# Macaron block: flag 2 summed in a gate bank, tile 2's norm moved to GpSimd with its own loads, the first norm in halves, and new orders on every engine

## The chip, the cores and the metric

One core of a Trainium2 chip. The metric is the device time of the kernel in microseconds (us); lower is better. The kernel before was run three times: 368.39, 368.41 and 369.13 us, median 368.41 us.

## What is computed

The input is 4096 tokens of 128 features (16 sequences of 256). Two feed-forward halves stand around an attention-like pooling, each with a residual and each behind a norm over the features:

```python
def ffn(x):                       # weights are -1, 0 or 1, with a scale per output
    h = silu(tlin(x, w1)) * tlin(x, w2)        # 128 -> 512, twice
    h = gelu(tlin(h, h1))                      # 512 -> 512
    h = gelu(tlin(h, h2))                      # 512 -> 512
    return tlin(h, w3)                         # 512 -> 128
x = x + 0.5 * ffn(layernorm(x))
h = layer_norm(layernorm(x), gamma, beta)      # keys, values, logits: 128 x 128
w = exp(key_att / sqrt(128)); w = w / cumsum(w, axis=1)
x = x + cumsum(w * keys, axis=1) * values
x = x + 0.5 * ffn(layernorm(x))
```

## The kernel before, in words

Tokens are cut into 8 tiles of 512. The feed-forward network runs 16 times: T = 0 to 7 is the first half, T = 8 to 15 the second, and `a0` to `a7` are the attention of the tiles between them. Activations stand with features on the partitions and tokens along the row, so one matmul has 128 x 512 moving elements. Each activation is split into a rounded part and its rest (`hi` and `lo`), and every product is two matmuls, one with each part, on a rounded copy of the weights.

The layers are called by the names that stand in the orders: `p1.m` is block m of the first layer (four matmuls: gate with hi and lo, up with hi and lo), `p2.m` and `p3.m` a block of the two 512-wide layers (8 matmuls), `p4` the last layer (8). ScalarE (ACT) computes `tanh`, `gelu2`, `gelu3` and the hi parts `high1` to `high3`; VectorE (DVE) computes `gate` and `up` (the silu product) and the lo parts `low1` to `low3`; GpSimd (POOL) takes the two lo parts `low1.1` and `low1.2` of the first tile and rounds the weights of h1, h2 and w3 (`hi`).

**Orders.** No scheduler runs. Each engine follows a list written out by hand: `START` has the stages before and during the first layer of tile 0, `SECOND_LAYER` has the matmuls of tile 0's second layer one by one (`p2ahi.0` is input block a, hi part, output block 0), and `STEPS` has 16 further steps. A prefix such as `0:` or `a1:` names another tile than the step's own. Every engine runs its list in order, so an instruction that waits holds all behind it.

**Norms.** Tiles 0, 1 and 2 (`BY_PE`) are normalised in the layout with tokens on partitions: DVE takes statistics (`stats`, `aggr`, `veps`), POOL the roots (`norm`, a power), ACT (for tile 0 mostly DVE) forms `z`, and four transposes on TensorE (PE) turn it (`t`). All other tiles go another way: POOL aggregates the statistics (`aggregate`), SP sends means and roots to DRAM (`park`) and back, spread over all partitions (`wide`), and POOL adds and multiplies (`xn.0`, `xn.1`) on the transposed input `xt_sb`, which arrives by one 2 MB load.

**Flags.** The kernel has two versions of each matmul, on rounded and on raw weights, and decides at run time: the low bits of the weights are looked at (`bits`), their maxima are summed over partitions by a 1-wide matmul (`flag:sum`), DVE copies the sum (`flag:copy`), and PE's sequencer loads it and branches. There are three such branches: before the first layer of tile 0, before its second layer, and before the rest. In this data the flags are 0. The sum of flag 2 is written in `y_ps`, which `p1.3` of tile 0 needs afterwards, so it stands between `p1.1` and `p1.2`, and `p1.3` waits for its copy:

```python
def flag_home(part):
    return (hid_ps[0], y_ps, xt_ps)[part - 1][0:1, 0:1]
...
if (T, m) in ((0, 3), (1, 1)):
    eng.wait_ge(s_flag, T + 2)
```

**Ahead of the first layer** PE runs seven `warm_up` matmuls on ones (two passes each): four at once, two after the variances (`s_ve`), one after the roots (`s_pow`); then the sum of flag 1 and the transposes of tile 0.

Of the kernel before, what the change touches and what calls it, by code (L numbers as in the profile page):

```python
# [36 lines left out]
    "DVE": (  # L37
        "stats aggr veps bits:w1 bits:w2 norm",
        "flag:copy1 bits:h1.0 t vec:scales bits:h1.2 stats flag:raise2 aggr gate.0 veps flag:copy2 up.0 gate.1 "
        "up.1 low1.0 gate.2 up.2 gate.3 up.3 bits:h2.1 low1.3 1:t",  # L40
# [32 lines left out]
        "a1:norm norm a1:xn.0 a0:weight a1:xn.1 xn.0 xn.1",
        "norm a0:dt xn.0 xn.1",
        "a2:norm a1:weight norm a2:xn.0 a2:xn.1 a1:dt xn.0 xn.1",
        "a3:norm norm a3:xn.0 a3:xn.1 a2:weight xn.0 xn.1",
        "a2:dt norm a4:norm xn.0 xn.1",
        "a3:weight norm a4:xn.0 a4:xn.1 xn.0 xn.1",
        "a5:norm a3:dt a4:weight a5:xn.0 a5:xn.1 norm a4:dt xn.0 xn.1",
# [1138 lines left out]
```

## Time and profile before

| | |
|---|---|
| median of three runs | 368.41 us |
| the profiled execution | 368.15 us |
| its span | 366.4 us |
| mean granted TensorE clock | 0.998 of full |
| PE busy | 359.3 us, 98% |
| DVE, ACT, POOL busy | 316.2, 283.1, 163.3 us |

A busy PE is not PE at its peak, since matmuls overlap and their ends are modelled; what shows a loss is the distance from one start to the next. The span lies 1.75 us below the execution's own time, and that rest lies outside of the profiled instructions.

### The profile page before, as it was taken

To read this page: it belongs to the slowest core of one execution; us is meant where nothing else is said; L and a number is where in the kernel's file an instruction comes from. 1 tells how busy PE (TensorE), PEld (TensorE's weight loads), DVE (VectorE), ACT (ScalarE), POOL (GpSimd) and SP (SyncE) were. 2 spreads that over 40 slices of the span, in tenths; PEclk is the share of its full clock that TensorE was granted. 3 is DMA by queue.
4 is the path that set the end of the run, shared out by engine and by line. 5 is a ranking of instruction groups with operands and counts; after the bars stand their busy time and mean duration, and the time that the engine had idled before them with its cause. 6 is when DMAs were issued, how large, how long until landed. Compare 5 with 4: busy or idle time off the path is not lost.

```text
span 366.4 us, 5194 instructions
## 1 busy us (share of the span) xinstructions
PE 359.3 (98%) x1578; PEld 285.1 (78%) x1578; DVE 316.2 (86%) x550; ACT 283.1 (77%) x465; POOL 163.3 (45%) x251
## 2 busy tenths in 40 slices
PE   7999999999999999999999999999999999999996
PEld 2678888787877777788778787787778777888885
DVE  5999688999989998889899989998899799857642
ACT  4998777987777879776887968877897697686763
POOL 3553344649045565812685545652573740530000
PEclk9999999999999999999999999999999999999999
DMA  7770103030100301300222012012022020040001
GB/s 245 270 294 4 54 3 107 8 110 9 58 2 0 86 29 36 83 0 2 59 59 59 1 59 59 0 59 86 0 59 88 2 86 2 4 111 2 1 30 63
DMA packets 16256, 20.94 MB, mean 57 GB/s; under 512 B 7008, under 2 KB 8288, under 8 KB 15968
## 3 DMA queue, kind: packets, MB, share of 16 engines
q1 hardware_dynamic: 15504, 19.75, 18.2%
q10 hardware_dynamic: 720, 0.80, 0.7%
q8 instruction: 16, 0.26, 0.3%
q14 instruction: 16, 0.13, 0.1%
HBM read 18.36 MB, written 2.18 MB: 56 GB/s over the span
## 4 chain that ended last, share of the span: by engine, by line
PE 96%; DVE 2%; issue 1%; ACT 1%; POOL 0%; POOLq 0%; ACTq 0%
PE hid_ps L643 62%; PE gate_ps L643 8%; PE y_ps L643 8%; PE up_ps L643 7%; PE y_ps L662 2%; PE xt_ps L829 2%; PE xt_ps L833 2%; PE xt_ps L836 2%; PE y_ps L843 1%; PE gate_ps L707 1%; PE up_ps L707 1%; DVE gate L1070 0%; PE xt_ps L643 0%; DVE xt_sb L1142 0%; PE xt_ps L656 0%
## 5 line engine op out<-in xcount | busy, mean ns | idle before, releaser
L643 PE MATMUL hid_ps<-act_hi,hi_h 128*128 128x512 f32 x480 | 193.3, 403 | 0.0
L643 PE MATMUL hid_ps<-act_lo,hi_h 128*128 128x512 f32 x480 | 186.7, 389 | 0.0
L1092 DVE TENSOR_TENSOR act_lo<-full,act_hi 128x512 fp32r<-128x512 f32 x185 | 132.8, 742 | 23.6 <-ACT act_hi L909 20.6
L902 ACT ACTIVATE full<-hid_ps,vec 128x512 f32<-128x512 f32 x123 | 84.1, 687 | 57.2 <-PE hid_ps L643 51.7
L643 PEld LDWEIGHTS hid_ps<-act_hi,hi_h 128*128 128x128 f32 x480 | 90.3, 188 | 22.8 <-issue 2.6
L643 PEld LDWEIGHTS hid_ps<-act_lo,hi_h 128*128 128x128 f32 x480 | 90.2, 188 | 21.3 <-issue 2.6
L909 ACT ACTIVATE act_hi<-full 128x512 fp32r<-128x512 f32 x127 | 78.6, 628 | 1.6
L567 POOL TENSOR_TENSOR xnt<-xt_sb,wide 128x512 f32<-128x512 f32 x21 | 29.4, 1400 | 45.8 <-DMA wide<-rows 45.8
L885 ACT ACTIVATE tanh<-gate_ps,s_half 128x512 f32<-128x512 f32 x60 | 40.4, 680 | 7.4 <-PE gate_ps L643 7.3
L1070 DVE SCALAR_TENSOR_TENSOR gate<-tanh,gate_ps 128x512 f32<-128x512 f32 x60 | 40.3, 674 | 6.5 <-ACT tanh L885 6.4
L1082 DVE SCALAR_TENSOR_TENSOR full<-up_ps,s_half,gate 128x512 f32<-128x512 f32 x60 | 44.1, 741 | 1.1
L890 ACT ACTIVATE act_hi<-full 128x512 fp32r<-128x512 f32 x60 | 36.9, 625 | 1.9 <-DVE full L1082 1.7
L573 POOL TENSOR_TENSOR xnt<-xnt,wide 128x512 f32<-128x512 f32 x21 | 30.0, 1428 | 3.2 <-POOL xnt L567 0.4
L622 POOL TENSOR_TENSOR xt_sb<-xt_sb,adelta 128x512 f32<-128x512 f32 x8 | 12.3, 1532 | 42.7 <-DVE adelta L1174 42.7
L540 POOL TENSOR_TENSOR pair_diff<-stats 128x4 f32<-128x4 f32 x21 | 8.2, 388 | 44.2 <-DVE stats L1040 44.2
L1158 DVE RECIPROCAL rcsum<-csum 128x256 f32<-128x256 f32 x16 | 27.8, 1740 | 0.0
L553 POOL TENSOR_TENSOR pair<-veps,half 128x4 f32<-128x4 f32 x21 | 26.1, 1244 | 3.3 <-POOL veps L550 0.4
L643 PE MATMUL gate_ps<-xn_hi,hi_w 128*128 128x512 f32 x59 | 25.1, 425 | 0.3 <-ACT full L902 0.3
L643 PE MATMUL y_ps<-act_hi,hi_w 128*128 128x512 f32 x60 | 23.8, 396 | 0.0
L643 PE MATMUL y_ps<-act_lo,hi_w 128*128 128x512 f32 x60 | 23.4, 390 | 0.0
L643 PE MATMUL gate_ps<-xn_lo,hi_w 128*128 128x512 f32 x59 | 23.0, 391 | 0.0
L643 PE MATMUL up_ps<-xn_hi,hi_w 128*128 128x512 f32 x59 | 23.0, 390 | 0.0
(170 smaller groups left out, 440.3 us busy)
## 6 DMA issues: line engine op xcount, KB each, us to landing
wide<-rows SPq DMA_DIRECT2D x42, 256.0 KB, 3.7
xt_sb<-xt SPq DMA_DIRECT2D x1, 2048.0 KB, 10.6
out<-xt_sb SPq DMA_DIRECT2D x7, 256.0 KB, 4.0
x_sb<-x SPq DMA_DIRECT2D x1, 1536.0 KB, 6.8
raw_h<-h2t SPq DMA_DIRECT2D x4, 256.0 KB, 7.1
raw_h<-h1t SPq DMA_DIRECT2D x2, 256.0 KB, 6.1
rows<-pair SPq DMA_DIRECT2D x21, 4.0 KB, 2.2
raw_w<-w2t ACTq DMA_DIRECT2D x1, 256.0 KB, 4.0
```

The costliest lines, as they stand in the source:

```text
L553: eng.tensor_tensor(pair_b[q][:, 1, :], veps[:, :], half[:, :], ALU.pow).then_inc(s_pow, 1)
L567: eng.tensor_tensor(xnt_b[i][:, :], xt_tile(t), wide_b[i][:, 0:TOK], ALU.add).then_inc(s_centred, 1)
L573: eng.tensor_tensor(xnt_b[i][:, :], xnt_b[i][:, :], wide_b[i][:, TOK:2 * TOK], ALU.mult).then_inc(s_xn, 1)
L643: mm = eng.matmul(ps, w, a, start=(first and n == 0), stop=(last and n == len(seq_) - 1))
L885: eng.activation(tanh_b[m % 2][:, :], gate_home(T, m)[:, :], ACT.Tanh, scale=s1_half[:, m:m + 1]).then_inc(s_tanh, 1)
L890: eng.activation(act_hi[first_act(T)][:, m, :], full1[m % 2][:, :], ACT.Copy).then_inc(s_hi[1], 1)
L902: eng.activation(full23[m % 2][:, :], home23(n, T, m)[:, :], ACT.Gelu, scale=col("sh1" if n == 2 else "sh2", m)).then_inc(s_gelu[n], 1)
L909: eng.activation(act_hi[n][:, m, :], full23[m % 2][:, :], ACT.Copy).then_inc(s_hi[n], 1)
L1070: eng.scalar_tensor_tensor(gate_b[m % 2][:, :], tanh_b[m % 2][:, :], 1.0, gate_home(T, m)[:, :], ALU.add, ALU.mult).then_inc(s_gate, 1)
L1082: eng.scalar_tensor_tensor(full1[m % 2][:, :], up_home(T, m)[:, :], s12_half[:, m:m + 1], gate_b[m % 2][:, :], ALU.mult, ALU.mult).then_in ...
L1092: eng.tensor_tensor(act_lo[a][:, m, :], full[m % 2][:, :], act_hi[a][:, m, :].bitcast(F32), ALU.subtract).then_inc(s_lo[n], 1)
L1158: eng.reciprocal(rcsum[:, b], csum[:, b]).then_inc(s_rc, 1)
```

## The change

- **Flag 2.** Its sum goes to `gate_ps[0]`, behind all of `p1.0` to `p1.3`, and waits for the first `gate` instead of `xn_lo`. `p1.3` of tile 0 no longer waits for a flag.
- **Tile 2.** `BY_PE` is now (0, 1): tile 2 goes by POOL, park and wide. Its `x` and its part of `xt` have loads and semaphores of their own, ahead of the rest; the other parts of `xt` follow in two loads.
- **First norm.** Aggregation, variances and roots of tile 0 are made in two halves, and DVE's `z` blocks wait for their half alone.
- **Weights.** The rounding of h2 and w3 on POOL is now part of the orders.
- **Orders.** All lists are written anew.

```diff
-        "p1.0 p1.1 flag:sum2 p1.2 p1.3",
+        "p1.0 p1.1 p1.2 p1.3 flag:sum2",
...
-        "hi:w1 hi:w2 z",
-        "t vec:s1 bits:h1.1 bits:h1.3 tanh.0 tanh.1 tanh.2 high1.0 tanh.3 high1.1 z.0 z.1 high1.2 bits:h2.0 "
-        "high1.3 1:t",
+        "hi:w1 hi:w2 z 0:t vec:s1",
+        "tanh.0 tanh.1 bits:h1.1 tanh.2 bits:h1.3 bits:h2.0 high1.0 tanh.3 high1.1 z.0 high1.2 z.1",
...
     "POOL": (
-        "norm",
-        "norm xn.0 xn.1",
+        "hi:h2.0 hi:h2.1 hi:h2.2 norm hi:h2.3 xn.0 xn.1",
+        "hi:w3 norm xn.0 xn.1",
...
-BY_PE = (0, 1, 2)
-AGGREGATE = 3
+BY_PE = (0, 1)
+AGGREGATE = 2
...
-            return (hid_ps[0], y_ps, xt_ps)[part - 1][0:1, 0:1]
+            return (hid_ps[0], gate_ps[0], xt_ps)[part - 1][0:1, 0:1]
...
-            xload(2, NT, s_xr)
+            xload(2, 3, s_x2t)
+            eng.dma_start(xt_tile(2), xt[:, 2 * TOK:3 * TOK]).then_inc(s_xt2, 16)
+            xload(3, NT, s_xr)
...
-            eng.dma_start(xt_sb[:, :], xt).then_inc(s_xt, 16)
+            eng.dma_start(xt_sb[:, 0:2 * TOK], xt[:, 0:2 * TOK]).then_inc(s_xt, 16)
+            eng.dma_start(xt_sb[:, 3 * TOK:], xt[:, 3 * TOK:]).then_inc(s_xt, 16)
...
+            def first_norm():
+                for h, ready, done in ((0, s_ve_first, s_pow_first), (1, s_ve, s_pow)):
+                    cut = slice(h * SUB // 2, (h + 1) * SUB // 2)
+                    eng.wait_ge(ready, 1)
+                    eng.tensor_tensor(rstd[:, cut], veps[:, cut], half[:, cut], ALU.pow).then_inc(done, 1)
+                eng.wait_ge(s_pow_first, 1)
+                eng.wait_ge(s_pow, 1)
+                eng.tensor_tensor(nmr[:, :], neg_mean[:, :], rstd[:, :], ALU.mult).then_inc(s_nmr, 1)
...
-                if (T, m) in ((0, 3), (1, 1)):
-
-                    eng.wait_ge(s_flag, T + 2)
+                if (T, m) == (1, 1):
+
+                    eng.wait_ge(s_flag, 3)
...
                 if part == 2:
-                    eng.wait_ge(s_xlo_half, 2)
+                    eng.wait_ge(s_gate, 1)
...
-                eng.wait_ge(s_pow, 1)
                 for j in range(SUB - act_z(0)):
+                    eng.wait_ge(*((s_pow_first, 1) if j < SUB // 2 else (s_pow, 1)))
```

What stands on PE in the first layer of tile 0. Before, from its second block to its end (the 1-wide matmul is the sum of flag 2):

```order
L643 MATMUL up_ps<-xn_hi,hi_w 128x512
L643 MATMUL up_ps<-xn_lo,hi_w 128x512
L764 MATMUL y_ps<-ones,inexact 1x1
L643 MATMUL hid_ps<-xn_hi,hi_w 128x512
L643 MATMUL hid_ps<-xn_lo,hi_w 128x512
```

Now, at the section's end (the branch to the flag's load follows at once):

```order
L659 MATMUL xt_ps<-xn_hi,hi_w 128x512
L659 MATMUL xt_ps<-xn_lo,hi_w 128x512
L780 MATMUL gate_ps<-ones,inexact 1x1
L871 UNCONDITIONAL_BRANCH
```

The sum moved from the middle of the section to behind its last product. On DVE, from the copy of flag 1 (`flag_i<-hid_ps`) to the copy of flag 2 (`flag_i<-y_ps`), before:

```order
L1027 CAST flag_i<-hid_ps 1x1
L1012 TENSOR_REDUCE bits<-raw_h 128x1
L1122 TENSOR_TENSOR xn_lo<-xt_ps,xn_hi 128x256
L1122 TENSOR_TENSOR xn_lo<-y_ps,xn_hi 128x256
...
L1012 TENSOR_REDUCE bits<-raw_h 128x1
L1040 BN_STATS stats<-x_sb 128x6 x4
L1022 TENSOR_REDUCE inexact<-bits 128x1
L1045 MEMSET fence 128x1
L1047 BN_AGGR mv<-stats 128x2 x4
L1070 SCALAR_TENSOR_TENSOR gate<-tanh,gate_ps 128x512
L1054 TENSOR_SCALAR neg_mean<-mv 128x4
L1055 TENSOR_SCALAR veps<-mv 128x4
L1027 CAST flag_i<-y_ps 1x1
```

Now, behind both `xn_lo`, up to the copy of flag 2 (`flag_i<-gate_ps`):

```order
L1026 TENSOR_REDUCE bits<-raw_h 128x1
L1013 TENSOR_SCALAR s_half<-vec 128x1
L1015 TENSOR_TENSOR s_half<-s_half,vec 128x4
L1026 TENSOR_REDUCE bits<-raw_h 128x1
L1090 SCALAR_TENSOR_TENSOR gate<-tanh,gate_ps 128x512
L1057 BN_STATS stats<-x_sb 128x6 x4
L1102 SCALAR_TENSOR_TENSOR full_0<-up_ps,s_half,gate 128x512
L1062 MEMSET fence 128x1
L1064 BN_AGGR mv<-stats 128x2 x4
L1036 TENSOR_REDUCE inexact<-bits 128x1
L1090 SCALAR_TENSOR_TENSOR gate<-tanh,gate_ps 128x512
L1041 CAST flag_i<-gate_ps 1x1
```

The first look at h1's bits moved behind `xn_lo`, and `up.0` and a second `gate` came in ahead of the copy. On ACT, behind tile 0's `xn_hi`, up to the first hi part of the activations. Before:

```order
L914 ACTIVATE keys,bits<-raw_h 128x512
L914 ACTIVATE csum,bits<-raw_h 128x512
L885 ACTIVATE tanh<-gate_ps,s_half 128x512 x2
L885 ACTIVATE tanh<-hid_ps,s_half 128x512
L890 ACTIVATE act_hi<-full_0 128x512
```

Now:

```order
L899 ACTIVATE tanh<-gate_ps,s_half 128x512 x2
L928 ACTIVATE keys,bits<-raw_h 128x512
L899 ACTIVATE tanh<-hid_ps,s_half 128x512
L928 ACTIVATE csum,bits<-raw_h 128x512
L928 ACTIVATE rcsum,bits<-raw_h 128x512
L904 ACTIVATE act_hi<-full_0 128x512
```

The two looks at h1's bits moved behind the first `tanh`, and a look at h2's bits came in ahead of `act_hi`.

## Rows read from the trace of the kernel before

**Rows 1.** Busy time of each engine in three stretches, with granted clock.

```profile
8.60:13.60 5.00, 4.45 (x22) 3.06 (x22) 4.96 (x22) 4.10 (x11) 2.96 (x5) 1.00 0.75 280
13.60:25.40 11.80, 11.49 (x50) 8.41 (x50) 11.24 (x29) 11.36 (x24) 7.44 (x9) 1.00 0.89 335
50.00:150.00 100.00, 100.00 (x434) 80.11 (x433) 93.61 (x154) 81.84 (x131) 55.64 (x91) 1.00 0.15 43
```

**Rows 2.** Timeline of PE, first layer: start us, duration, instruction, idle before.

```profile
6.65 0.81 PE L843 MATMUL y_ps<-ones 128*1 128x256 f32 x3
...
8.69 0.36 PE L678 MATMUL gate_ps<-xn_hi,hi_w 128*128 128x256 f32 x1 [0.56 <-ACT xn_hi L968]
...
10.42 0.40 PE L643 MATMUL up_ps<-xn_lo,hi_w 128*128 128x512 f32 x1
...
11.22 0.50 PE L643 MATMUL hid_ps<-xn_hi,hi_w 128*128 128x512 f32 x1
...
13.04 0.39 PE L643 MATMUL xt_ps<-xn_lo,hi_w 128*128 128x512 f32 x1
13.64 0.47 PE L707 MATMUL gate_ps<-act_hi,hi_h 128*128 128x512 f32 x1 [0.22 <-ACT act_hi L890]
```

**Rows 3.** Load of flag 1 by PE's sequencer: durations in ns, start.

```profile
L856 PEldq TENSOR_LOAD <-flag_i x1: 492/492/492, 7.8 to 7.8; - x1
```

**Rows 4.** Timeline of DVE, from the first variances to the second gate.

```profile
5.18 1.27 DVE L1012 TENSOR_REDUCE bits<-raw_w 128x1 f32<-128x512 uint16 x2
...
7.58 0.15 DVE L1027 CAST flag_i<-hid_ps 1x1 int32<-1x1 f32 x1 [0.30 <-PE hid_ps L756]
...
8.70 0.41 DVE L1122 TENSOR_TENSOR xn_lo<-y_ps,xn_hi 128x256 fp32r<-128x256 f32 x1
...
9.46 0.68 DVE L1012 TENSOR_REDUCE bits<-raw_h 128x1 f32<-128x512 uint16 x1
10.12 0.87 DVE L1040 BATCH_NORM_STATS2 stats<-x_sb 128x6 f32<-128x128 f32 x4
...
12.76 0.66 DVE L1070 SCALAR_TENSOR_TENSOR gate<-tanh,gate_ps 128x512 f32<-128x512 f32 x1
```

**Rows 5.** Timeline of ACT: a look at bits of h1.

```profile
8.88 0.63 ACT L914 ACTIVATE keys<-raw_h 128x512 f32<-128x512 uint16 x1 [0.18 <-DMA raw_h<-h1t]
```

**Rows 6.** Timeline of POOL: a power, and the rounding of h2.

```profile
5.36 1.02 POOL L578 TENSOR_TENSOR rstd<-veps,half 128x4 f32<-128x4 f32 x1 [3.30 <-DVE veps L1055]
...
18.27 2.76 POOL L584 CAST hi_h<-raw_h 128x512 fp32r<-128x512 f32 x4
```

**Rows 7.** Timeline of PE: first layer of tile 1, tile 2's transposes.

```profile
25.50 0.47 PE L643 MATMUL gate_ps<-xn_hi,hi_w 128*128 128x512 f32 x1 [0.32 <-ACT full L902]
...
26.86 0.49 PE L643 MATMUL hid_ps<-act_hi,hi_h 128*128 128x512 f32 x1
...
30.63 0.60 PE L656 MATMUL xt_ps<-ident,z 128*128 128x128 f32 x4
30.98 0.48 PE L643 MATMUL hid_ps<-act_hi,hi_h 128*128 128x512 f32 x1
```

**Rows 8.** Tile 3's norm: first and last of the aggregation, `xn.0`, `xn.1`.

```profile
30.02 0.21 POOL L540 TENSOR_TENSOR pair_diff<-stats 128x4 f32<-128x4 f32 x1 [4.71 <-DVE stats L1040]
...
32.07 1.04 POOL L553 TENSOR_TENSOR pair<-veps,half 128x4 f32<-128x4 f32 x1
...
38.73 1.29 POOL L567 TENSOR_TENSOR xnt<-xt_sb,wide 128x512 f32<-128x512 f32 x1 [5.62 <-DMA wide<-rows]
40.17 1.56 POOL L573 TENSOR_TENSOR xnt<-xnt,wide 128x512 f32<-128x512 f32 x1
```

**Rows 9.** SP's issues of the load of `xt` and of tile 3's first `wide`.

```profile
16.05 0.45 SPq L486 DMA_DIRECT2D xt_sb<-xt  x1
...
34.73 0.34 SPq L503 DMA_DIRECT2D wide<-rows  x1
```

**Rows 10.** Issues of DMA by line: KB each, us from issue to landing.

```profile
xt_sb<-xt SPq DMA_DIRECT2D x1, 2048.0 KB, 10.6
```

More of the change, by code:

```diff
@@ L29 @@
         "flag:sum1 t",
-        "p1.0 p1.1 flag:sum2 p1.2 p1.3",
+        "p1.0 p1.1 p1.2 p1.3 flag:sum2",
     ),
     "ACT": (
-        "hi:w1 hi:w2 z",
-        "t vec:s1 bits:h1.1 bits:h1.3 tanh.0 tanh.1 tanh.2 high1.0 tanh.3 high1.1 z.0 z.1 high1.2 bits:h2.0 "
-        "high1.3 1:t",
+        "hi:w1 hi:w2 z 0:t vec:s1",
+        "tanh.0 tanh.1 bits:h1.1 tanh.2 bits:h1.3 bits:h2.0 high1.0 tanh.3 high1.1 z.0 high1.2 z.1",
     ),
     "DVE": (
-        "stats aggr veps bits:w1 bits:w2 norm",
-        "flag:copy1 bits:h1.0 t vec:scales bits:h1.2 stats flag:raise2 aggr gate.0 veps flag:copy2 up.0 gate.1 "
-        "up.1 low1.0 gate.2 up.2 gate.3 up.3 bits:h2.1 low1.3 1:t",
[4 rows of a table added]
     ),
@@ L51 @@
     "SP": (
-        "",
+        "park wide",
         "park wide",
         "a0:park a0:wide park wide",
-        "a1:park park a1:wide wide",
-        "park wide",
-        "a2:park park a2:wide wide",
+        "a1:park a1:wide park",
+        "park 5:wide wide",
+        "a2:park a2:wide park wide",
         "a3:park a3:wide park wide",
@@ L62 @@
         "park wide",
-        "a6:park 8:store a6:wide park wide",
-        "a7:park a7:wide 9:store park wide",
-        "10:store park 11:store wide store",
+        "a6:park a6:wide park wide",
+        "a7:park a7:wide park 8:store wide",
+        "park 9:store 10:store 11:store wide store",
         "store",
@@ L69 @@
     "POOL": (
-        "norm",
-        "norm xn.0 xn.1",
+        "hi:h2.0 hi:h2.1 hi:h2.2 norm hi:h2.3 xn.0 xn.1",
+        "hi:w3 norm xn.0 xn.1",
         "a0:norm norm a0:xn.0 a0:xn.1 xn.0 xn.1",
[L73 to L79, printed above, removed]
+        "a1:norm norm 6:norm a1:xn.0 a0:weight a1:xn.1 xn.0 xn.1",
+        "a0:dt a1:weight xn.0 xn.1",
+        "a2:norm norm a2:xn.0 a2:xn.1 xn.0 a1:dt xn.1",
+        "a3:norm norm a3:xn.0 a2:weight a3:xn.1 xn.0 xn.1",
+        "a2:dt norm a4:norm a3:weight xn.0 xn.1",
+        "norm a4:xn.0 a4:xn.1 a3:dt xn.0 xn.1",
+        "a5:norm a4:weight a5:xn.0 a5:xn.1 norm a4:dt xn.0 xn.1",
         "norm a5:weight xn.0 xn.1",
@@ L304, in macaron_block @@
         s_x0_half, s_xt = sem("s_x0_half"), sem("s_xt")
+        s_x2t, s_xt2 = sem("s_x2t"), sem("s_xt2")
         s_h1 = [sem(f"s_h1_{k}") for k in range(MC)]
@@ L387, in items @@
                     yield stage, chunk, int(which) if which else i + AHEAD.get(stage, 0)
-        norm_of = {("ffn", t): t for t in range(2)}
-        for i, order in enumerate(STEPS["DVE"]):
+        norm_of = {}
+        for i, order in enumerate(START["DVE"] + STEPS["DVE"], -2):
             for stage, _, t in items(order, i):
                 if stage in ("stats", "att_stats"):
-                    norm_of["ffn" if stage == "stats" else "att", t] = len(norm_of)
+                    norm_of.setdefault(("ffn" if stage == "stats" else "att", t), len(norm_of))
         assert len(norm_of) == 3 * NT
@@ L562, in xn_add @@
                     eng.wait_ge(s_x1, t + 1)
+                elif t == 2:
+                    eng.wait_ge(s_xt2, 16)
                 elif t < NT:
-                    eng.wait_ge(s_xt, 16)
+                    eng.wait_ge(s_xt, 32)
                 else:
@@ L592, in low1 @@
                                   ALU.subtract).then_inc(s_lo[1], 1)
-            norm(0)
+            first_norm()
             eng.wait_ge(s_z, SUB - 1)
@@ L602, in _ @@
                     low1(stage)
-            for k in range(MC):
-                hi("h2", k)
-            hi("w3", 0)
             def emit(stage, chunk, t):
-                if stage in ("norm", "att_norm"):
+                if stage == "hi":
+                    hi(t, chunk or 0)
+                elif stage in ("norm", "att_norm"):
                     kind = "ffn" if stage == "norm" else "att"
@@ L796, in emit @@
                             return
-                        free("xt", (s_xlo, t))
-                        transpose4(xt_ps, z, s_t)
                     elif stage == "p4":
@@ L1027, in copy_flag, with blocks_of, norm_stats @@
                 eng.tensor_copy(flag_i[0:1, part - 1:part], home).then_inc(s_flag, 1)
-            def norm_stats(kind, t):
+            def blocks_of(half):
+                return range(SUB) if half is None else range(half * SUB // 2, (half + 1) * SUB // 2)
+            def norm_stats(kind, t, half):
                 n = norm_of[kind, t]
@@ L1036, in norm_stats @@
                     eng.wait_ge(s_nmr, n - LINES + 1)
-                for j in range(SUB):
+                for j in blocks_of(half):
                     if (n, j) == (0, SUB // 2):
@@ L1040, in norm_stats, with norm_aggr, norm_veps @@
                     eng.bn_stats(stats_b[n % LINES][:, j, :], norm_blk(kind, t, j)).then_inc(s_bn, 1)
-            def norm_aggr(n):
-                eng.wait_ge(s_bn, SUB * n + SUB)
+            def norm_aggr(n, half):
+                eng.wait_ge(s_bn, SUB * n + blocks_of(half)[-1] + 1)
                 eng.memset(fence[:, :], 0.0)
-                for j in range(SUB):
+                for j in blocks_of(half):
                     eng.bn_aggr(mv[:, j, :], stats_b[n % LINES][:, j, :]).then_inc(s_mv, 1)
-            def norm_veps(n):
-                eng.wait_ge(s_mv, SUB * n + SUB)
+            def norm_veps(n, half):
+                js = blocks_of(half)
+                cut = slice(js[0], js[-1] + 1)
+                eng.wait_ge(s_mv, SUB * n + js[-1] + 1)
                 if n > 0:
                     eng.wait_ge(s_nmr, n)
-                eng.tensor_scalar(neg_mean[:, :], mv[:, :, 0], -1.0, None, ALU.mult)
-                eng.tensor_scalar(veps[:, :], mv[:, :, 1], 1.0, EPS, ALU.mult, ALU.add).then_inc(s_ve, 1)
+                eng.tensor_scalar(neg_mean[:, cut], mv[:, cut, 0], -1.0, None, ALU.mult)
+                eng.tensor_scalar(veps[:, cut], mv[:, cut, 1], 1.0, EPS, ALU.mult,
+                                  ALU.add).then_inc(s_ve_first if half == 0 else s_ve, 1)
             def first_norm():
-                eng.wait_ge(s_pow, 1)
                 for j in range(SUB - act_z(0)):
+                    eng.wait_ge(*((s_pow_first, 1) if j < SUB // 2 else (s_pow, 1)))
                     eng.tensor_scalar(z[:, j * P:(j + 1) * P], norm_blk("ffn", 0, j), mv[:, j, 0:1], rstd[:, j:j + 1],
@@ L1145, in emit @@
                     if t == 0:
-                        eng.wait_ge(s_xt, 16)
+                        eng.wait_ge(s_xt, 32)
                     eng.wait_ge(s_p4, t + 1)
```

13 lines of the change are left out of this document (7 added, 6 removed), and 184 rows, old and new, of tables (SECOND_LAYER, START, STEPS).

## The prediction

> **What bounds the kernel now.** I read the page first, then the busy time by stretches. From 50 to 150 us PE is busy for 100.00 of 100.00 us at the full clock [rows 1], and the two stretches of 100 us behind it read the same. So no engine but PE can give time there, and no order can: what is left to gain is in the start. In the first 5 us of the first layer PE is busy for 4.45, while DVE is for 4.96; from 13.60 to 25.40 PE lacks 0.31 of 11.80 [rows 1]. The end time is therefore PE's fixed work plus PE's pauses, nearly all of them ahead of 26 us, and I sum pauses.
>
> The reader is to see these in PE's timeline [rows 2]. A 512-wide matmul starts 0.23 behind the one before it. From 10.42 to 11.22 there are 0.80, so 0.57 are lost at the sum of flag 2. From 13.04 to 13.64 there are 0.60, so 0.37 are lost at the first `act_hi`. Ahead of 8.69 the warm-up matmuls run without a gap up to about 7.46 (0.81 from 6.65), and the flag's sum and the transposes follow. The copy of flag 1 ends at 7.58 + 0.15 = 7.73 [rows 4], the load of it begins at 7.8 and takes 0.49 [rows 3], and the first matmul comes at 8.69: 0.96 from copy to matmul, although `xn_hi` was there earlier. A flag read with nothing queued on PE behind it costs this 0.9 to 1.0. The Trainium skill (DMA: Bandwidth & Descriptors, Latency and other measured facts) gives such a load a floor of about 600 ns; this trace's 0.49 is below it, so the row stands, and by the page the sum at the end would be 0.1 more. Later, at 25.50, PE waits once more, for ACT [rows 7].
>
> **The first norm in halves: +0.1.** The start of `z` is not bound by the roots alone: DVE looks at w1 and w2 until 5.18 + 1.27 = 6.45, and the power ends at 5.36 + 1.02 = 6.38 [rows 4, 6]. The change puts a memset and two short instructions more ahead of these looks, with a wait between them. I take 0.3 to 0.4 for it, from the distance of such instructions (the aggregation to the looks at 5.18), so `z` comes at 6.8 instead of 6.4. PE doesn't care: its warm-ups hold it until 7.46. But the second part of the warm-ups waits for the variances, whose semaphore now comes 0.3 later; it had some 0.1 of slack. What I add is 0.1. The cost of a power on half the columns isn't in the trace: between nearly nothing and the whole 1.02 [rows 6]. I take about 0.6, since four columns took 1.02 and POOL's other instructions on as few columns take 0.2, so most of it goes with the columns. At the whole price, twice, the last warm-up waits until 7.4 and the start comes 0.4 later; below zero there is nothing, since the warm-ups stand.
>
> **Flag 2: the pause moves and grows, +1.5 at the start of the second layer.** The 0.57 at 10.42 go. `p1.3` then ends its issue at 12.5 instead of 13.3. But the read of flag 2 was hidden before: its copy stood ahead of `up.0` and so ahead of the second gate at 12.76 [rows 4], while PE had matmuls until 13.04 [rows 2]. Now nothing is queued on PE behind the sum. So I follow DVE, which copies it, in its new order. Both `xn_lo` end at 8.70 + 0.41 + 0.1 = 9.2. Then: look at h1 0.67, scales 0.4, look 0.67 (the distance from 9.46 to 10.12), which gives 10.95; gate 0.66; statistics 0.8 (the row's 0.87 ends 0.1 into the next instruction), `up` 0.7, aggregation 0.35, raise 0.1: 13.5; the second gate 0.66 and the copy: 14.25 [rows 4]. The first `tanh` is no bound (done at 10.6, as its bank is done at 9.9). On ACT the looks at h1 come behind the `tanh`s (0.63 each, with 0.78 to the next start [rows 5]); the last ends at 13.3, just ahead of the raise. From the copy 0.85 to 0.95 to PE's first matmul (the 0.96 above; two waits follow the branch): 15.1. `act_hi` isn't later: a look at h2 from 13.3, then `act_hi` until 14.7. So the second layer starts at 15.1 against 13.64, and behind the DVE's queue are `veps`, `up.1` and `low1.0`, which come 1 us later too.
>
> **From there to the second layer's end: +1.0 left.** Fewer pauses are left, because PE comes later than its inputs. I went through the new list with steps of 0.23: `low1.0` is done at 15.8 for its place at 15.9, POOL's `low1.1` at 17.3 for 17.8, `z` at 18.6 for 18.9, `low1.2` at 19.2 for 19.4. All are in time by 0.1 to 0.5. PE reaches tile 1's `p1.3` at 26.7; its banks are free when two `gelu2` are done, which stand on ACT behind the `tanh` of `p1.1`'s bank (24.8, three times 0.68): 26.9. Before it was 25.50 [rows 7], so +1.4. The fold's matmuls, which stood between 26.4 and 26.86, now lie ahead of `p1.3` and no longer behind it. So the first `p3` comes at 27.85 against 26.86 [rows 7]: +1.0.
>
> **Tile 2's transposes: -0.4.** Four starts from 30.63 to 30.98 go, 0.35 [rows 7], and the matmul behind transposes is a little slow. ACT is rid of four `z` (1.6 us), DVE of `aggr` and `veps`; both are off PE's path there, which is worth nothing with PE at 100%.
>
> **Tile 2 by POOL: 0.** Its chain is: `low1.2` until 19.2, three roundings of 0.69 (2.76 for four [rows 6]) until 21.3, aggregation 3.1 (30.02 to 33.11 [rows 8]) until 24.4. Then park. Tile 3 took 1.6 from the end of its power to the first `wide` (34.73 [rows 9]) and 4.0 more to `xn.0` at 38.73 [rows 8]. But the load of `xt` runs from 16.05 to 26.65 (10.6 [rows 9, 10]), and park is issued in the midst of it. I take it to land as that load ends: `wide` at 27.0, `xn.0` 31.0, `xn.1` done 34.0 (3.0 for both [rows 8]), ACT's `xn_hi` 34.6, `xn_lo` 35.3. PE wants the one at 27.85 + 4 x 1.81 = 35.1 and the other at 35.3. So it just fits; the bounds are 0 and 1.2. The roundings of h2 that wait behind the aggregation end at 25.1, ahead of the first `p3`.
>
> **All other orders: 0**, with bounds 0 and +0.8: PE is full there, so a new order can only bring a wait in.
>
> **The sum.** +1.0 - 0.4 + 0 = +0.6, of which +0.1 is the norm's. Against the profiled execution, 368.15 (span 366.4 and 1.75 around it), that is 368.7. The median of the runs is 0.26 above that execution, so 368.9 to 369.0; I take 368.9. A measurement of this kernel can tell about 0.2% (0.7 us) from no change.
>
> **A: as summed, 45%.** Own range 368.3 to 369.7, since the start at 15.1 is known to about 0.3 and the stretch behind it to 0.4. The bound of 0.2% at 369.15 cuts it: same 27, slower 18.
>
> **B: a new wait at tile 2 or in the orders, 20%.** Place: `p1.0` of tile 2, at 35 us. It decides if park's 4 KB wait longer than until 26.65 or if `wide` needs more than 4.0. Each us of lateness is one of PE's: 0.7 to 1.5 more, so 369.6 to 370.4. For it: 0.0 to 0.1 of slack in my sum. Against it: landing without the load's queue would be a us sooner. The Trainium skill (DMA: Bandwidth & Descriptors, section Two DMAs through the same engine are not ordered) says that descriptors of one queue start in order, which speaks for this rival, since park would start behind the whole load.
>
> **C: faster, 20%.** The second layer starts at 13.7 or sooner. Place: the copy of flag 2 on DVE. It decides if that copy ends by 12.9 instead of 14.25. Then the pauses of 0.57 and 0.37 are gone for good, the transposes' 0.4 and part of the wait at 25.50 too: 1.0 to 1.4 less, 367.0 to 367.4. For it: all the gaps that it closes are there [rows 2]. Against it: DVE was busy for 4.96 of 5.00 us [rows 1], and `up` and a second gate were put ahead of the copy. Faster 18, same 2.
>
> **D: PE's clock falls in the pause, 5%.** PE stands still from 12.9 to 15.1, 2.2 us, where it never stood longer than 0.6 behind the warm-ups [rows 2]; the granted clock was full all along [rows 1]. At the lower of its two levels, 1.2 instead of 2.4 GHz, each us of the time costs half a us. I take 4 us for it, a guess below the 6.65 by which the warm-ups had brought it up [rows 2], so 2 us: 370.9. The Trainium skill (TensorE: Matmul & The Clock Gate, What's actually happening) has the clock follow PE's recent activity, which is this rival's ground.
>
> **E: half a power costs a whole one, 5%.** 0.4 more: 369.3, slower 4, same 1. **F: no effect, 5%.** The flag's gain and its price cancel, 367.6 to 368.4: same 4, faster 1. Of B, 18 are slower and 2 the same.
>
> Together, rounded: faster (18 + 1) 0.20, same (27 + 2 + 2 + 1 + 4) 0.35, slower (18 + 18 + 5 + 4) 0.45. The range: 367.4 to 370.6; it leaves out the better half of C and D, and the end of B.
>
> **What would show it.** Right: no gap at 10.4; the second layer's first matmul at 15.1; `p1.3` of tile 1 at 26.9; the first `p3` at 27.9; no transposes at 31; PE full from 28 us on. Wrong: a copy of flag 2 ahead of 13.5; a flag read under 0.7; a wait of PE at 35 us on `xn_hi` or `xn_lo`; a granted clock under 1 at 15 us; waits of PE behind 50 us.

## The result: 369.84 us against 368.40, and the profile after

Over 12 runs each the changed kernel takes 369.84 us in the median (368.62 to 370.80), the kernel before 368.40 (367.54 to 369.58): a ratio of 1.0038, interval 1.0029 to 1.0047, so 1.4 us slower. The profiled execution took 369.77 us with a span of 368.0, 1.6 more than before's.

The first view is PE's timeline, cut to the places that matter: start, duration, instruction, idle time ahead.

```profile
9.15 0.35 PE L694 MATMUL gate_ps<-xn_hi,hi_w 128*128 128x256 f32 x1 [0.60 <-ACT xn_hi L982]
...
12.69 0.39 PE L659 MATMUL xt_ps<-xn_lo,hi_w 128*128 128x512 f32 x1
13.63 0.19 PE L780 MATMUL gate_ps<-ones,inexact 128*1 128x1 f32 x2 [0.55 <-DVE inexact L1036]
14.87 0.47 PE L723 MATMUL gate_ps<-act_hi,hi_h 128*128 128x512 f32 x1 [1.05 <-ACT act_hi L904]
...
26.75 0.47 PE L659 MATMUL gate_ps<-xn_hi,hi_w 128*128 128x512 f32 x1
...
27.75 0.39 PE L659 MATMUL hid_ps<-act_hi,hi_h 128*128 128x512 f32 x1
...
35.02 0.39 PE L659 MATMUL gate_ps<-xn_hi,hi_w 128*128 128x512 f32 x1
35.52 0.50 PE L659 MATMUL gate_ps<-xn_lo,hi_w 128*128 128x512 f32 x1
...
332.28 0.41 PE L659 MATMUL gate_ps<-xn_hi,hi_w 128*128 128x512 f32 x1
332.86 0.50 PE L659 MATMUL gate_ps<-xn_lo,hi_w 128*128 128x512 f32 x1 [0.17 <-DVE xn_lo L1147]
```

Against [rows 2]: the first layer is dense now and ends at 12.69 instead of 13.04 although it begins 0.46 later, but the second begins 1.23 later, at 14.87. Against [rows 7]: the two places come 1.25 and 0.89 later. The transposes of tile 2 are gone, which gives back 0.44. Then come two waits that before doesn't have. At 35.02 and at 332.28 a matmul is followed by the next after 0.50 and 0.58 instead of 0.23. Both times it waits for `xn_lo`, of tile 2 and of the last tile.

To follow the loss further, count PE's matmuls back from the end in both traces and compare the starts of those with as much work behind them. The changed kernel is 0.30 later behind tile 2's place (0.89 at the first `p3`, less 0.44 for the transposes, less 0.15 since its matmuls lie a little closer there), 0.73 behind 35, 0.80 at 100, 1.20 behind a wait at 136.41 (DVE's `act_lo`), 1.33 from 225 on and 1.79 behind 332. That is the loss, by place: 0.3 in the start, 0.4 at tile 2, 1.1 in the other orders. Towards the end 0.17 comes back, which leaves the span's 1.6.

Next DVE's timeline of the changed kernel ahead of the second layer:

```profile
11.04 0.69 DVE L1090 SCALAR_TENSOR_TENSOR gate<-tanh,gate_ps 128x512 f32<-128x512 f32 x1 [0.16 <-ACT tanh L899]
11.65 0.86 DVE L1057 BATCH_NORM_STATS2 stats<-x_sb 128x6 f32<-128x128 f32 x4
12.43 0.73 DVE L1102 SCALAR_TENSOR_TENSOR full<-up_ps,s_half,gate 128x512 f32<-128x512 f32 x1
...
13.49 0.68 DVE L1090 SCALAR_TENSOR_TENSOR gate<-tanh,gate_ps 128x512 f32<-128x512 f32 x1
14.08 0.14 DVE L1041 CAST flag_i<-gate_ps 1x1 int32<-1x1 f32 x1
```

POOL's timeline of it for tile 2, from the casts of h2 to the first addition, and the same addition of the last tile:

```profile
18.98 2.19 POOL L602 CAST hi_h<-raw_h 128x512 fp32r<-128x512 f32 x3
21.14 0.20 POOL L547 TENSOR_TENSOR pair_diff<-stats 128x4 f32<-128x4 f32 x1
...
30.90 1.29 POOL L576 TENSOR_TENSOR xnt<-xt_sb,wide 128x512 f32<-128x512 f32 x1 [6.54 <-DMA wide<-rows]
...
328.63 1.29 POOL L576 TENSOR_TENSOR xnt<-xt_sb,wide 128x512 f32<-128x512 f32 x1 [7.17 <-DMA wide<-rows]
```

And SP's (the DMA queue's own; the second number is the time to issue), at tile 2 and at the last tile:

```profile
23.81 0.39 SPq L502 DMA_DIRECT2D rows<-pair  x1
27.43 0.34 SPq L510 DMA_DIRECT2D wide<-rows  x1
...
321.48 0.37 SPq L502 DMA_DIRECT2D rows<-pair  x1
321.90 1.44 SPq L520 DMA_DIRECT2D out<-xt_sb  x3
324.45 0.33 SPq L510 DMA_DIRECT2D wide<-rows  x1
```

The same places for the last tile in the kernel before, SP's issues and POOL's first addition:

```profile
319.10 0.37 SPq L495 DMA_DIRECT2D rows<-pair  x1
319.51 0.47 SPq L513 DMA_DIRECT2D out<-xt_sb  x1
320.70 0.32 SPq L503 DMA_DIRECT2D wide<-rows  x1
...
325.31 1.84 POOL L567 TENSOR_TENSOR xnt<-xt_sb,wide 128x512 f32<-128x512 f32 x1 [6.24 <-DMA wide<-rows]
```

The copy of flag 2 ends at 14.22 (14.25 in the prediction), and the matmul follows 0.65 behind it. From tile 2's park to its `wide` 3.62 us pass, from the last tile's 2.97, with three stores between the two. In the kernel before both took 1.6, tile 3's in [rows 9] and the last tile's here, with one store between.

### The profile page after: what moved, and what is told of

It reads as the page before. It is cut to its first block, busy times and chain, and to the rows that moved or that the text cites. A ratio compares the mean times of both kernels' runs of the same rounds, so it can differ in the third digit from the quotient of the medians.

```text
span 368.0 us, 5197 instructions
## 1 busy us (share of the span) xinstructions
PE 359.8 (98%) x1574; PEld 284.5 (77%) x1574; DVE 316.5 (86%) x546; ACT 281.6 (77%) x461; POOL 171.5 (47%) x260
## 4 chain that ended last, share of the span: by engine, by line
PE 84%; DMA 4%; POOL 4%; DVE 3%; issue 2%; ACT 2%; POOLq 0%; ACTq 0%; DVEq 0%; SPq 0%
PE hid_ps L659 54%; PE gate_ps L659 7%; PE y_ps L659 7%; PE up_ps L659 7%; PE y_ps L678 2%; DMA wide<-rows 2%; PE xt_ps L843 2%; PE xt_ps L847 2%; PE xt_ps L850 2%; DMA rows<-pair 2%; PE y_ps L857 2%; POOL xnt L576 1%; DVE act_lo L1112 1%; DVE gate L1090 1%; POOL hi_h L602 1%
## 5 line engine op out<-in xcount | busy, mean ns | idle before, releaser
L576 POOL TENSOR_TENSOR xnt<-xt_sb,wide 128x512 f32<-128x512 f32 x22 | 31.9, 1452 | 46.3 <-DMA wide<-rows 46.2
L582 POOL TENSOR_TENSOR xnt<-xnt,wide 128x512 f32<-128x512 f32 x22 | 30.9, 1406 | 2.7
L659 PE MATMUL gate_ps<-xn_hi,hi_w 128*128 128x512 f32 x59 | 25.9, 439 | 0.0
L659 PE MATMUL up_ps<-xn_lo,hi_w 128*128 128x512 f32 x59 | 23.0, 390 | 0.0
```

What stands on the lines that cost most here:

```text
L576: eng.tensor_tensor(xnt_b[i][:, :], xt_tile(t), wide_b[i][:, 0:TOK], ALU.add).then_inc(s_centred, 1)
L582: eng.tensor_tensor(xnt_b[i][:, :], xnt_b[i][:, :], wide_b[i][:, TOK:2 * TOK], ALU.mult).then_inc(s_xn, 1)
L659: mm = eng.matmul(ps, w, a, start=(first and n == 0), stop=(last and n == len(seq_) - 1))
```

## Experiments

Twelve kernels in four groups, each with the kernel before on the same chip (medians of before 368.50, 368.19, 368.48 and 368.17). Ratios are to before, with their 95% interval. Kernels that differ by one or two thousandths aren't told apart by their times; there the traces show which wait is there and which isn't.

### Parts of the change, one at a time

**Flag 2 alone.** Before, with only this, and the two waits that go with it (`p1.3` of tile 0 no longer waits for the flag, the sum waits for the first `gate`):

```diff
-        "p1.0 p1.1 flag:sum2 p1.2 p1.3",
+        "p1.0 p1.1 p1.2 p1.3 flag:sum2",
...
-            return (hid_ps[0], y_ps, xt_ps)[part - 1][0:1, 0:1]
+            return (hid_ps[0], gate_ps[0], xt_ps)[part - 1][0:1, 0:1]
...
-        "flag:copy1 bits:h1.0 t vec:scales bits:h1.2 stats flag:raise2 aggr gate.0 veps flag:copy2 up.0 gate.1 "
+        "flag:copy1 bits:h1.0 t vec:scales bits:h1.2 stats flag:raise2 aggr gate.0 veps up.0 gate.1 flag:copy2 "
```

> The kernel before with one thing moved: flag 2 is summed behind p1.3 in the first gate bank and copied behind gate.1; all orders else are before's. Theory (the flag's place costs little, what follows it costs): the 0.57 us gap at 10.42 goes, the copy lands near 13.3 and the second layer starts at 13.8 to 13.9 instead of 13.64, so the kernel is within 0.3 us of before (368.4 to 368.8). Rival (the late read itself is the loss of the changed kernel's start): the second layer starts at 14.7 or later and the kernel costs 0.9 us or more over before.

368.60 us, ratio 0.9995 (0.9983 to 1.0007). The second layer starts at 13.68, 5.06 behind the first matmul (4.95 before), and PE runs 0.39 ahead of before until 210; 0.33 of that is lost by 225. The theory holds, the late read is not the loss: with before's orders around it the copy is early enough, and the 0.57 at 10.42 and a wait of 0.22 for `act_lo` are gone.

**The first norm whole.** The changed kernel, one power on POOL again, for which all of DVE's `z` wait, and

```diff
-        "stats.0 stats.1 aggr.0 veps.0 aggr.1 veps.1 bits:w1 bits:w2 norm flag:copy1 0:t bits:h1.0 vec:scales",
+        "stats aggr veps bits:w1 bits:w2 norm flag:copy1 0:t bits:h1.0 vec:scales",
```

> The changed kernel with the first norm's aggregation, variances and roots whole again. Theory (the half norm makes the first matmul 0.46 us late, by a late variance semaphore and by powers of 0.69 us each): the first first-layer matmul starts near 8.7 instead of 9.15, and as the flag's copy and the act_hi behind it follow it, the kernel gets 0.3 to 0.45 us faster than the changed one (369.4 to 369.5). Rival (x landed 0.2 us later and the vector engine's order is what counts): the matmul stays at 8.95 or later, gain 0.2 us at most.

369.72 us, 1.0030 (1.0018 to 1.0042): no gain. The first matmul came at 8.41 and the second layer 0.74 sooner than in the changed kernel's trace, and then it was lost at once, as PE's timeline of this kernel shows:

```profile
12.89 0.19 PE L780 MATMUL gate_ps<-ones,inexact 128*1 128x1 f32 x2 [0.55 <-DVE inexact L1036]
14.13 0.47 PE L723 MATMUL gate_ps<-act_hi,hi_h 128*128 128x512 f32 x1 [1.04 <-ACT act_hi L904]
...
17.14 0.63 PE L723 MATMUL up_ps<-act_hi,hi_h 128*128 128x512 f32 x1
17.56 0.63 PE L723 MATMUL gate_ps<-act_hi,hi_h 128*128 128x512 f32 x1
17.99 0.63 PE L723 MATMUL gate_ps<-act_lo,hi_h 128*128 128x512 f32 x1
18.41 0.44 PE L723 MATMUL up_ps<-act_lo,hi_h 128*128 128x512 f32 x1
```

Matmuls start 0.43 apart instead of 0.23. The busy times by stretch of the same kernel say why (busy time and count of PE, PEld, DVE, ACT, POOL, then granted clock, DMA share, GB/s):

```profile
9.00:14.00 5.00, 3.53 (x19) 2.59 (x18) 4.87 (x21) 4.42 (x11) 1.40 (x4) 1.00 0.64 218
14.00:19.00 5.00, 4.87 (x14) 3.73 (x15) 4.93 (x11) 4.46 (x10) 4.20 (x6) 0.66 0.88 305
19.00:26.00 7.00, 7.00 (x35) 5.50 (x34) 4.85 (x10) 4.68 (x9) 4.30 (x11) 1.00 0.92 340
```

The granted clock is 0.66 over 14 to 19, so PE was at the lower of its two levels for more than half of that stretch, behind its pause from 12.35 to 14.13. PE went from 0.74 ahead of the changed kernel to 0.87 behind: 1.6 us. That is rival D, and it comes and goes between executions of one kernel (below). The first norm itself can't be priced from this time, so neither theory nor rival is decided.

**Flag 2 copied sooner**, by the orders:

```diff
-        "tanh.0 tanh.1 bits:h1.1 tanh.2 bits:h1.3 bits:h2.0 high1.0 tanh.3 high1.1 z.0 high1.2 z.1",
+        "bits:h1.1 tanh.0 tanh.1 bits:h1.3 tanh.2 high1.0 tanh.3 high1.1 z.0 high1.2 z.1 bits:h2.0",
-        "stats.0 stats.1 aggr.0 veps.0 aggr.1 veps.1 bits:w1 bits:w2 norm flag:copy1 0:t bits:h1.0 vec:scales",
-        "bits:h1.2 gate.0 stats up.0 aggr flag:raise2 gate.1 flag:copy2 veps up.1 low1.0 gate.2 up.2 gate.3 "
+        "stats.0 stats.1 aggr.0 veps.0 aggr.1 veps.1 bits:w1 bits:w2 norm flag:copy1 bits:h1.0 0:t vec:scales",
+        "bits:h1.2 stats gate.0 aggr up.0 flag:raise2 gate.1 flag:copy2 veps up.1 low1.0 gate.2 up.2 gate.3 "
```

> The changed kernel with flag 2 copied sooner: bits h1.1 go into ScalarE's 1.2 us of idle time ahead of the first tanh, bits h2.0 behind z, bits h1.0 into the vector engine's idle time ahead of xn_lo, up.0 and the flag ahead of the rest. Theory (the second layer waits for the copy and for an act_hi that stand behind checks which could lie elsewhere): the copy lands at 13.4 to 13.6 instead of 14.08, the second layer starts at 14.0 to 14.3 instead of 14.87, the kernel is 0.5 to 0.9 us faster than the changed one (368.9 to 369.3). Rival (what is won at the second layer's start is given back at its act_lo or its later flag): the start moves, p1.3 of tile 1 stays at 26.7, and the time stays at 369.8.

369.85 us, 1.0032 (1.0015 to 1.0050). The copy came at 13.07 and the second layer at 13.90, 4.93 behind the first matmul instead of 5.71, and `p3` at 27.08, not 27.75. But `xn_lo` of tile 2 was ready only at 35.1, so PE's matmul there came 0.52 late instead of 0.27, and about 0.6 were lost at 260 and 0.3 at 332. The theory was right on the start, which can be had from the orders. The rival was right on the time, since the gain was given back, but not on the place: `p1.3` of tile 1 did come sooner, and the loss is at tile 2, which doesn't follow, and behind.

**Part of `xt` later.** The 1280 KB transfer is issued behind tile 2's `wide`:

```diff
-            eng.dma_start(xt_sb[:, 3 * TOK:], xt[:, 3 * TOK:]).then_inc(s_xt, 16)
...
                     wide("ffn" if stage == "wide" else "att", t)
+                    if (stage, t) == ("wide", 2):
+                        eng.dma_start(xt_sb[:, 3 * TOK:], xt[:, 3 * TOK:]).then_inc(s_xt, 16)
```

> The changed kernel with the 1280 KB transfer of xt issued behind tile 2's wide rows instead of ahead of the steps. Theory (the park of tile 2 is slow since it shares the queues with that transfer): park to wide takes 1.6 to 2.5 us instead of 3.6, wide is issued 1 us or more sooner, PE's wait at 35 (0.38 us) goes, and the kernel is 0.3 to 0.4 us faster than the changed one (369.4 to 369.5). Rival (the park is slow whatever lies beside it, or the 3.6 us are the park's turn behind GpSimd): the wait at 35 stays within 0.1 us of what it is, and so does the time.

369.19 us, 1.0020 (1.0004 to 1.0036). Park to `wide` took 3.24 instead of 3.62, and the wait at 35 stayed (0.29). The theory was not confirmed. Only the 512 KB of `xt` were still under way when park was issued at 23.47, and they landed at 24.10, 2.6 before park did. So what held it is not seen here; the 1280 KB account for 0.4 at most.

### Tile 2 and the later orders

**The aggregation ahead of the casts**, in POOL's first step:

```diff
-        "hi:h2.0 hi:h2.1 hi:h2.2 norm hi:h2.3 xn.0 xn.1",
+        "norm hi:h2.0 hi:h2.1 hi:h2.2 hi:h2.3 xn.0 xn.1",
```

> The changed kernel with GpSimd's aggregation of tile 2 ahead of its three casts of h2 (2.2 us) instead of behind them. Theory (tile 2's xn is late since its aggregation stands behind casts that nothing waits for before 26.7): the park is issued near 21.7 instead of 23.8, tile 2's xn_lo is ready by 34, PE's wait at 35 (0.38 us) goes, the kernel is 0.3 to 0.4 us faster than the changed one. Rival (the path is bound by the DMA queues, which carry xt until 27.1): the park is issued earlier, the wide rows land at 30.5 to 30.9 all the same, and the wait at 35 stays.

369.59 us (7 runs), 1.0044 (1.0026 to 1.0062). Park was issued 2 us sooner, at 21.85, and `wide` at 26.56: 4.71 for 4 KB. PE's wait at 35 is gone in this trace, since `xn_lo` came 0.8 sooner, and the median didn't fall. In the kernels below with the same edit, both together and both with the earlier copy, the park took 5.51 and 6.83. However early it is issued, from 20.9 to 23.8, `wide` comes between 26.6 and 27.7. That is what the rival said of the queue, though the wait did not stay.

**Before's orders from step 4 on**: on all five engines the strings of the steps from the fifth on are those of the kernel before; what the two versions do before that point is the same set of operations, but for POOL's norm 6 and DVE's `dt` of tile 2.

> The changed kernel with the orders of before on all five engines from step 4 (near 70 us) on; what comes ahead of it is the changed kernel's. Theory (the other orders lose by themselves, at PE's waits at 136 and 332 and by some hundredths elsewhere): 0.5 to 0.9 us faster than the changed one (368.9 to 369.3), with a PE timeline that runs parallel to before's behind 75. Rival (those waits are chance of one execution, and the loss lies in the first 50 us): no more than 0.2 us faster.

369.76 us, 1.0041 (1.0026 to 1.0055). The clock fell in the profiled execution (0.69 over 14 to 19) and in 3 more of 10. Behind 105 the difference to before stays between 2.46 and 2.50 up to the end: the wait at 332 isn't there, which the traces with the new orders have. But where the two sets of orders join, PE loses 0.6 at 104, where it waits for DVE's `up`; neither set has that alone. So the time says nothing on the theory; the trace supports it for 332.

**Both**, and **both with the earlier copy**:

> Both of the two kernels above together: tile 2's aggregation first, before's orders from step 4 on. Theory: the two shares add, 0.8 to 1.3 us faster than the changed one (368.5 to 369.0), what is left over before is the start's 0.45 us less rounding. Rival (one wait takes up what the other gives): no faster than the better of the two alone.

For both together 370.44 us (6 runs), 1.0058 (1.0040 to 1.0075): the clock fell (0.66), the join cost 0.6, and waits near 237 took 0.77 more. A miss.

> The three together: flag 2 copied sooner as in the run above with the second layer at 13.9, tile 2's aggregation first, before's orders from step 4 on. Theory (the earlier start was only lost to the waits at 35, 260 and 332): the first third-layer matmul 0.2 us behind before's, no wait at 35, the transposes' 0.44 us kept, so 368.1 to 368.5, level with before or up to 0.3 us faster. Rival (the earlier start is taken up by another wait whatever the orders): 368.8 or more.

With the earlier copy as well 369.39 us, 1.0037 (1.0019 to 1.0055). The second layer started at 13.46 and `p3` 0.19 ahead of before; then PE stood 1.10 at 33.7 for `xn_hi` of tile 2, because of the park of 6.83. The rival.

### The queue, the idle stretch, the repairs

**The queue clear for the parks.** The aggregation first, and

```diff
-            eng.dma_start(xt_sb[:, 0:2 * TOK], xt[:, 0:2 * TOK]).then_inc(s_xt, 16)
-            eng.dma_start(xt_sb[:, 3 * TOK:], xt[:, 3 * TOK:]).then_inc(s_xt, 16)
...
                     wide("ffn" if stage == "wide" else "att", t)
+                    if (stage, t) == ("wide", 2):
+                        eng.dma_start(xt_sb[:, 0:2 * TOK], xt[:, 0:2 * TOK]).then_inc(s_xt, 16)
+                        eng.dma_start(xt_sb[:, 3 * TOK:], xt[:, 3 * TOK:]).then_inc(s_xt, 16)
...
-        "park 9:store 10:store 11:store wide store",
+        "park wide 9:store 10:store 11:store store",
```

> The changed kernel with tile 2's aggregation ahead of the h2 casts, both transfers of xt (512 and 1280 KB) issued behind tile 2's wide rows, and the three stores near the end issued behind the last tile's wide rows instead of between its park and them. Theory (a 4 KB park lands only when what was queued ahead of it has drained: bulk xt at tile 2, 768 KB of stores at the last tile): tile 2's park takes 1.6 to 2.2 us instead of 4.7, its xn_lo is ready by 31, the last tile's park takes 1.6 to 2.0 us instead of 2.97, and PE's waits at 35 and at 332 (about 0.4 us each in the executions so far) are both gone; 0.6 to 0.9 us faster than the changed kernel (369.0 to 369.2 where before is at 368.5). Rival (these parks are slow for another reason, such as what DVE and GpSimd do): the two parks stay above 2.5 us and the waits stay.

368.82 us, 1.0021 (1.0004 to 1.0038). SP's timeline of this kernel at the two places:

```profile
22.01 0.39 SPq L500 DMA_DIRECT2D rows<-pair  x1
23.59 0.34 SPq L508 DMA_DIRECT2D wide<-rows  x1
...
320.35 0.37 SPq L500 DMA_DIRECT2D rows<-pair  x1
322.84 0.32 SPq L508 DMA_DIRECT2D wide<-rows  x1
```

And PE's, where the waits had been:

```profile
34.78 0.39 PE L660 MATMUL gate_ps<-xn_hi,hi_w 128*128 128x512 f32 x1
35.01 0.39 PE L660 MATMUL gate_ps<-xn_lo,hi_w 128*128 128x512 f32 x1
...
331.15 0.39 PE L660 MATMUL gate_ps<-xn_hi,hi_w 128*128 128x512 f32 x1
331.38 0.39 PE L660 MATMUL gate_ps<-xn_lo,hi_w 128*128 128x512 f32 x1
```

And POOL's first addition for the two tiles:

```profile
29.12 1.29 POOL L577 TENSOR_TENSOR xnt<-xt_sb,wide 128x512 f32<-128x512 f32 x1 [4.88 <-DMA wide<-rows]
...
326.75 1.29 POOL L577 TENSOR_TENSOR xnt<-xt_sb,wide 128x512 f32<-128x512 f32 x1 [6.43 <-DMA wide<-rows]
```

Tile 2's park takes 1.58 instead of 4.71, with the same aggregation and the same casts, and 1.58 and 1.69 in the two other kernels with this edit: what was slow is the loads of `xt` ahead of it. But of the 3.8 us by which `wide` is issued sooner than in the changed kernel only 1.8 arrive. `wide` now has the loads of `xt` right behind it, and from its issue to POOL's addition 5.5 us pass instead of 3.5. So `xn_lo` was ready at 34.46 and not by 31 as expected, which is 1.0 sooner than in the changed kernel and only 0.2 sooner than with the aggregation alone.

The last tile's park takes 2.49, also more than expected. What tells there is the whole way from the park's issue to the landing of `wide`: 6.7 to 7.2 us in the six traces with three stores between the two, 6.2 to 6.3 in the six with the stores behind `wide` or with before's later orders, 6.1 in before and with flag 2 alone. Its `xn_lo` starts at 330.23 and PE needs it at 331.38. Both waits are gone, and the profiled execution took 368.20, level with before's 368.15.

**The idle stretches filled**: the changed kernel with matmuls that compute nothing, `fill(1)` ahead of flag 2's sum and `fill(4)` behind it:

```diff
+            def fill(n):
+                for _ in range(n):
+                    eng.matmul(up_ps[0][0:1, 0:seq], ones[:, 0:1], ones[:, :], start=True, stop=True)
```

> The changed kernel with five matmuls of 256 columns that compute nothing, put into PE's two idle stretches ahead of the second layer: one before flag 2's sum, four behind it. Theory (it is the two idle stretches together, 0.94 and 1.2 us, after which the granted clock falls to half in some executions, near 15.1 to 18.6; it fell in 13 of 58 executions of the kernels with this start, and in none of 67 of before and of the kernel with flag 2 alone): the mean clock of every execution stays at 0.998 or more, and the time is 0 to 0.3 us below the changed kernel's. Rival (the clock falls for a reason outside the start, or the filling is too little): 2 or 3 of 12 executions show 0.993 to 0.995 again.

370.19 us (6 runs), 1.0052 (1.0039 to 1.0066), the clock never below 0.998. Each of the four came as two records, 1.89 us together, so the second layer started only at 15.60: +0.7, a mistake in size. With 6 runs, where the clock fell in one of five without the filling, it proves nothing on the clock.

**All together with before's front**: the clear queue, before's first orders with the first norm whole, flag 2 as in the first experiment.

> The first of these kernels with the start of the kernel with flag 2 alone: the first norm whole, the orders of before up to gate 3 of tile 0 on ScalarE and the vector engine, flag 2 in the gate bank behind p1.3. Theory (the losses are separate and each has been named: the second layer's start, tile 2's park, the last tile's park): second layer at 13.7, first third-layer matmul within 0.2 us of before's, the four transposes' 0.44 us kept, no wait at 35 or 332; 0.3 to 0.6 us faster than before. Rival (the later orders cost about 0.3 us at waits near 136 and 260, or a new wait follows where the start is earlier): level with before within 0.2 us or slower.

368.69 us, 1.0006 (0.9995 to 1.0016): the rival. No wait at 35 or 332, one of 0.26 at 136. The first matmul came at 9.41 and the second layer 5.29 behind it.

**Three repairs**: clear queue, earlier copy, first norm whole.

> The kernel with the queue clear for the parks, and with it the earlier copy of flag 2 (ScalarE's and the vector engine's orders of that run) and the first norm whole. From the traces so far: first matmul of the first layer to second layer 4.9 us instead of 5.72 (so 0.8 us sooner), vector engine's z 0.14 us sooner after x has landed, no wait at 35 or 332, clock never or nearly never falling since the idle stretches are shorter. Theory (the changed kernel's losses are the late flag copy with what stands ahead of it, tile 2's park and the last tile's park, and they add): 0.5 to 0.9 us faster than the kernel with the queue clear alone, so 0.1 to 0.5 us faster than before. Rival (waits near 136 and 260, which come and go between executions, take up an earlier start, as in the run with the earlier copy): level with before within 0.2 us, or no gain over the kernel with the queue clear.

368.46 us, 1.0005 (0.9994 to 1.0017). First matmul to second layer 4.88, as expected, no wait at 35, park 1.58, the clock at 0.998 or more in all 12. Yet it is level with before and not ahead of it, as the rival had it; in the profiled execution the warm-ups ended late (below), and 0.3 were lost at 136. No kernel here beats the one before.

## Why the prediction came out 0.9 too low

**The outcome** lies within the stated range (367.4 to 370.6) only because the range took in rival B. The main case, A, had 368.3 to 369.7; 369.84 is B's time (369.6 to 370.4), at B's place and further on in the orders. Two of the signs of being wrong came: a wait of PE at 35 us and waits behind 50.

**What bounds it** was right: PE's work is fixed, and the time follows its pauses one for one.

**The first norm in halves (+0.1)** was right in mechanism. From the landing of x (DVE's first statistics) to the first `z` 2.84 us pass in the nine traces with halves (2.87 in one), 2.70 in the five without: +0.14. The part of the warm-ups that waits for the variances starts 1.80 behind the first statistics instead of 1.61, so 0.2 later where I had 0.3. A half power takes 0.71 (0.6 in the prediction). What it costs at PE's first matmul is not shown: the +0.46 of this trace holds it together with an x that landed 0.21 later and warm-ups that ran slow for longer (last section).

**Flag 2 (+1.5 at the second layer)** measured +1.23. The mis-sized term is the read: from the end of the copy to the matmul 0.63 to 0.69 us pass in all twelve traces in which the matmul follows it at once, where I had 0.85 to 0.95 from flag 1. The load of flag 2 itself is shorter than flag 1's 0.49 [rows 3], which before's trace had already shown:

```profile
L856 PEldq TENSOR_LOAD <-flag_i x1: 307/307/307, 12.5 to 12.5; - x1
```

In all seven traces with this start it is 5.71 or 5.72 from the first matmul to the second layer. The price isn't the flag's: with before's orders around it it was 5.06 (5.29 in the kernel with everything together), with the copy brought forward 4.93 and 4.88. Nor is it `up.0` and the second `gate`, which stand ahead of the copy with before's orders too. It is what the new orders moved into DVE's and ACT's busy stretch: DVE's look at h1 behind `xn_lo`, the statistics behind the first `gate`, ACT's looks between the `tanh`s. Moving these gave 0.8 us; which of them counts most isn't separated. `p1.3` was forecast at 26.9 and came at 26.75, `p3` at 27.85 and 27.75, the transposes' -0.4 was -0.44, and 0.15 more came back in `p3`. So the start's +0.6 was +0.3.

**Tile 2 by POOL (0)** is the first step that failed: "So it just fits". It was rival B, at the place it named: `xn_lo` was ready at 35.46 (forecast 35.3) and PE's need was at 35.25; with the matmul behind the wait, +0.4. The landing assumed for park, the end of the load of `xt` at about 27, was right to 0.4. What I mis-sized was the slack: none, with a `wide` whose issue moves between 26.6 and 27.7. The Trainium skill (DMA: Bandwidth & Descriptors, Two DMAs through the same engine are not ordered) has descriptors of one queue start in order. These runs agree as far as 4.71 us with the bulk ahead and 1.58 without go; the 3.24 with only 512 KB ahead, landed 2.6 us before park did, is not explained by that order alone.

**All other orders (0)** is the second, and the larger: +1.1 in this trace, where I had 0.8 as the bound. I read nothing there but that PE was full, and didn't look at SP's list, in which three stores instead of one now stood between the last tile's park and its `wide`. The wait at 332 is that: with the matmul behind it 0.3 to 0.5 in five of the six traces with these later orders and this list, 0.1 in the sixth, none in the three with the stores moved. The new orders had also left little room there: `xn_lo` was ready 1.2 us ahead of PE's need with before's later orders, whatever the park took (1.5 to 2.7), and 0.5 with the new ones and the stores moved. The waits at 136 and 260 come in some traces only, and in the kernels with before's later orders others came, at 217 and 237. Why a given one comes in a given execution stays open.

In medians: the clear queue takes the ratio from 1.0038 to 1.0021, the start's repair on top to 1.0005. So about half of the 1.4 us lay in each; the intervals are as wide as these steps, so no finer split is shown.

**Rival D (5%)** was no rival but a lottery. The mean granted clock of an execution was 0.993 to 0.995 in 14 of 70 executions of the seven kernels with the changed start, in 2 of 35 with the earlier copy, in none of 24 with before's front and in none of 95 of before. In the three traces in which it fell, it fell behind a pause of 1.8 us with one tiny matmul in it (the stretch 14 to 19 above), and cost 1.6 us each, where I had guessed 2. Once in 12 runs of the changed kernel it moves the median little. The Trainium skill (TensorE: Matmul & The Clock Gate, What's actually happening) has the clock follow PE's recent activity. The counts agree in the main, since it fell most often where PE paused longest; but they are no clean order, since it fell twice in 35 with a pause of 0.9 to 1.0 us and never in 24 with one of 1.1 or 1.4.

The traces show one thing more. By the traces' record of the granted clock it had risen at 4.84, 5.15 and 5.64 us in the three executions in which it fell later, at 15.08, 15.39 and 15.88. In the eleven others it rose at 5.64 (the kernel with the stretches filled) to 7.98, and didn't fall. So in these traces a fall behind the pause goes with an early rise, and the rise differs from execution to execution. Three falls are few, and what links the two is open.
